# Two attention layers of a decoder on one core: key transfers moved from SyncE to GpSimd, and a causal mask moved from TensorE to VectorE

## The reference

```python
x = x + _L0_attn_ref(_layernorm(x), ...)           # causal, rotary factor on q and k
x = x + _L0_xattn_ref(_layernorm(x), ctx, ctx, ctx)  # a gated feed-forward on the context
x = x + _L0_ffn_ref(_layernorm(x), ...)            # experts
x = x + _L1_attn_ref(_layernorm(x), ...)           # full attention
x = x + _L1_xattn_ref(_layernorm(x), ctx, ...)     # cross attention, softmax over the queries
x = x + _L1_ffn_ref(_layernorm(x), ...)            # experts

def _L0_attn_ref(x, W_attn, b_attn, W_proj, b_proj):
    q, k, v = split(x @ W_attn.T + b_attn)         # 16 heads of 16
    att = (q * f) @ (k * f).T / sqrt(16)
    att = where(tril, att, finfo.min)
    return softmax(att) @ v @ W_proj.T + b_proj
```

## Time and profile before

| | us |
|---|---|
| median of 3 runs (lowest, highest) | 1650.03 (1648.86, 1650.86) |
| the profiled execution's own time | 1650.47 |
| its span | 1648.7 |
| layer 0's attention | about 5 to 280 |
| its context block and experts | 280 to 670 |
| layer 1's self-attention (b = 0 to 3) | 680 to 966 |
| its cross batches (b = 4 to 7) | 966 to 1204 |
| its experts | from 1209 |

### The profile page before, as it was taken

How to read it: one execution, slowest core, us unless ns; L and a number is a source line. 1 busy time by engine, 2 the same in 40 slices (tenths; PEclk the granted TensorE clock), 3 DMA queues, 4 the chain that set the end, 5 groups by cost and what they waited for, 6 DMA issues and landing times. The chain is left out here.

```text
span 1648.7 us, 30586 instructions
## 1 busy us (share of the span) xinstructions
PE 1464.2 (89%) x10430; PEld 1013.4 (61%) x10430; DVE 1165.7 (71%) x2116; ACT 900.5 (55%) x1704; POOL 561.3 (34%) x773
## 2 busy tenths in 40 slices
PE   7899998989899999688999998796965899999996
PEld 3455554559899998333434433232344899999996
DVE  4566553554778887477878759696858688888884
ACT  1354454123256665045666688686922566767662
POOL 6444530010235655545445442021013132333221
PEclk8799999999899999779999999898897999999998
DMA  6222220220258886532223222222133677787772
GB/s 165 50 50 57 47 56 2 73 93 33 103 156 256 255 238 161 133 74 56 57 41 72 55 56 47 61 52 61 40 103 112 221 224 240 240 238 227 252 220 42
DMA packets 104408, 194.48 MB, mean 118 GB/s; under 512 B 30432, under 2 KB 55904, under 8 KB 101312
## 3 DMA queue, kind: packets, MB, share of 16 engines
q1 hardware_dynamic: 75328, 157.91, 30.8%
q0 software_dynamic: 28416, 34.25, 11.9%
q10 hardware_dynamic: 512, 0.40, 0.1%
HBM read 135.76 MB, written 18.61 MB: 94 GB/s over the span
## 5 line engine op out<-in xcount | busy, mean ns | idle before, releaser
L807 ACT ACTIVATE l1a_sb_probs<-l1a_s_ps,l1a_sb_kmax 128x512 f32<-128x512 f32 x256 | 172.4, 700 | 41.4 <-DVE l1a_sb_kmax L740 40.2
L740 DVE TENSOR_REDUCE l1a_sb_kmax<-l1a_s_ps 128x1 f32<-128x512 f32 x256 | 160.5, 676 | 47.8 <-PE l1a_s_ps L932 47.2
L705 DVE TENSOR_REDUCE l1a_sb_mx<-l1a_s_ps 128x2 f32<-128x1024 f32 x128 | 153.4, 1218 | 42.1 <-PE l1a_s_ps L891 42.1
L813 ACT ACTIVATE l1a_sb_probs<-l1a_s_ps 128x1024 f32<-128x1024 f32 x128 | 130.1, 1024 | 85.1 <-PE l1a_s_ps L932 84.8
L932 PEld LDWEIGHTS l1a_s_ps<-l1a_sb_qst,l1a_sb_kst 49*128 49x128 f32 (+1 forms) x512 | 49.8, 193 | 171.5 <-issue 92.7
L705 DVE TENSOR_REDUCE l0a_sb_mx<-l0a_s_ps 128x2 f32<-128x256 f32 (+3 forms) x128 | 103.6, 821 | 72.5 <-PE l0a_s_ps L904 70.9
L2021 PE MATMUL l1m_g_ps<-l1m_sb_rows_hi,l1m_sb_hi 128*128 128x256 f32 x512 | 146.3, 286 | 2.1 <-DVE l1m_sb_late L1919 1.4
L2021 PE MATMUL l1m_g_ps<-l1m_sb_rows_lo,l1m_sb_hi 128*128 128x256 f32 x512 | 144.9, 283 | 0.0
L2021 PE MATMUL l1m_g_ps<-l1m_sb_rows_hi,l1m_sb_lo 128*128 128x256 f32 x512 | 144.9, 283 | 0.0
L932 PE MATMUL l1a_s_ps<-l1a_sb_qst,l1a_sb_kst 49*128 49x512 f32 (+1 forms) x512 | 129.3, 512 | 17.5 <-ACT l1a_sb_probs L807 15.6
L1893 DVE TENSOR_TENSOR l1m_sb_lo<-l1m_sb_raw,l1m_sb_hi 128x512 fp32r<-128x512 f32 x184 | 119.8, 693 | 18.5 <-ACT l1m_sb_hi L1804 17.4
(11 more groups left out here) (409 smaller groups left out, 3967.7 us busy)
## 6 DMA issues: line engine op xcount, KB each, us to landing
l1m_sb_raw<-in_l1m_w SPq DMA_DIRECT2D x92, 512.0 KB, 4.4
l0m_sb_raw<-in_l0m_w SPq DMA_DIRECT2D x72, 512.0 KB, 4.9
l1m_sb_raw<-in_l1m_w SPq DMA_DIRECT2D x23, 1024.0 KB, 6.4
l1a_sb_qst<-l1a_sb_hi SPq DMA_DIRECT2D x256, 32.0 KB, 2.0
l1a_sb_kst<-l1a_sb_hi POOLq DMA_DIRECT2D x156, 32.0 KB, 2.0
l0a_sb_qst<-l0a_sb_hi SPq DMA_DIRECT2D x128, 32.0 KB, 2.2
l1a_sb_qst<-l1a_sb_lo SPq DMA_DIRECT2D x128, 32.0 KB, 2.1
l0a_sb_kst<-l0a_sb_hi POOLq DMA_DIRECT2D x124, 32.0 KB, 2.0
```

What stands on the lines that cost most here:

```text
L705: dve.tensor_reduce(mx[:, g, qt, 2 * p:2 * p + 2], buffer("A", b, g, j)[:, :, 0:last], AX.X, ALU.max).then_inc(a_max.sem, 1)
L740: dve.tensor_reduce(kmax[:, n % 4, e:e + 1], buffer("S", b, g, j)[:, e, :], AX.X, ALU.max, negate=True).then_inc(kmax_done.sem, 1)
L807: ins = act.activation(probs[:, n % 8, e, :], at[:, e, :], ACT.Exp, bias=kmax[:, n % 4, e:e + 1], accum_out=zsum[:, n % 4, e:e + 1])
L813: act.activation(probs[:, n % 8, :, c0:T], at[:, :, c0:T], ACT.Exp, scale=SCALE).then_inc(exp_done.sem, 1)
```

## The change

There are two parts.

The transfers: the step STACK now stands for the queries alone, on SyncE; a new step KEYS, one for each head, issues that head's three key transfers from GpSimd, for all batches (by_sp and its semaphores are gone). In self-attention KEYS stands where STACK stood. The queries' STACK for group 0 of the next batch stands two score steps earlier, at j = 1 of group 1, ahead of M at j = 3. In the cross batches one head's KEYS stands in each of the steps 19 to 30 (groups 0 to 2 of the next batch), and in steps 0 to 3 (group 3 of the running one). CTX stands ahead of the queries' STACK in step 0.

The mask of layer 0: scores_by_query computes scores only. row_max becomes two instructions tensor_tensor_reduce, one for each head: they add a piece of a mask above (128 by 512, f32) to the scores, write the sum to seen (SBUF) and its maximum to mx. The constant mask_q is no longer loaded and cast; above is loaded in its place.

```diff
@@ self_slot
             if g >= 2 and nxt is not None:
                 yield "STACK", nxt, g - 1, 0
+                yield from keys(nxt, g - 1)
...
+        if j == 1 and g == 1 and nxt is not None:
+            yield "STACK", nxt, 0, 0
         if j == 3 and g == 1 and nxt is not None:
-            yield "STACK", nxt, 0, 0
+            yield from keys(nxt, 0)
@@ cross_slot
         if at == 0:
-            yield "STACK", b, NG - 1, 0
             if nxt is not None:
                 if not turned:
                     yield "LN2", nxt, 0, 0
                 yield "CTX", nxt, 0, 0
+            yield "STACK", b, NG - 1, 0
...
+        if at < GH:
+            yield "KEYS", b, NG - 1, at
+        if at >= 19 and nxt is not None and at < 19 + 3 * GH:
+            yield "KEYS", nxt, *divmod(at - 19, GH)
@@ SyncE, stack
-                if by_sp(b):
-                    hi_done.wait(sp, b, i + 1)
-                    lo_done.wait(sp, b, i + 1)
-                    for p in (2 * g, 2 * g + 1):
-                        for e in range(2):
-                            for n, source in enumerate((hi, hi, lo)):
-                                sp.dma_start(in_stack(kst, p, e, n), in_part(source, i + 1, p, e)
-                                             ).then_inc(kstacked_sp[p], 16)
@@ GpSimd
-            def stack(b, g, _):
-                if by_sp(b):
+            def stack(b, g, head):
+                p, e, i = 2 * g + head // 2, head % 2, 2 * (g // 2) + 1
+                if b == 0 and g == 0 and e:
                     return
-                i = 2 * (g // 2) + 1
                 hi_done.wait(pool, b, i)
                 lo_done.wait(pool, b, i)
                 s_ready.wait(pool, b - 1, 8 * g + 7)
-                for p in (2 * g, 2 * g + 1):
-                    for e in range(1 if b == 0 and g == 0 else 2):
-                        for n, source in enumerate((hi, hi, lo)):
-                            pool.dma_start(in_stack(kst, p, e, n), in_part(source, i, p, e)).then_inc(kstacked[p], 16)
+                for n, source in enumerate((hi, hi, lo)):
+                    pool.dma_start(in_stack(kst, p, e, n), in_part(source, i, p, e)).then_inc(kstacked[p], 16)
@@ VectorE, row_max
-                last = (qt + 1) * P if causal else T
-                dve.tensor_reduce(mx[:, g, qt, 2 * p:2 * p + 2], buffer("A", b, g, j)[:, :, 0:last], AX.X, ALU.max
+                if causal:
+                    last = (qt + 1) * P
+                    a_max.wait(dve, b, 8 * g + j - 2)
+                    for e in range(2):
+                        ins = dve.tensor_tensor_reduce(seen[:, j % 2, e, 0:last], buffer("A", b, g, j)[:, e, 0:last],
+                                                       above[:, T - last:T], 1.0, -3e38, ALU.add, ALU.max,
+                                                       mx[:, g, qt, 2 * p + e:2 * p + e + 1])
+                    ins.then_inc(a_max.sem, 1)
+                    return
+                dve.tensor_reduce(mx[:, g, qt, 2 * p:2 * p + 2], buffer("A", b, g, j)[:, :, :], AX.X, ALU.max
                                   ).then_inc(a_max.sem, 1)
@@ TensorE, scores_by_query
-                                    start=True, stop=not causal)
-                if causal:
-                    if b == 0 and g == 0 and j == 0:
-                        pe.wait_ge(const["halved"], 5)
-                    ins = masked(at[:, :, qt * P:last], "mask_q")
+                                    start=True, stop=True)
                 ins.then_inc(a_ready.sem, 1)
```

More of the change, by code:

```diff
@@ L99, in keep_warm, with keys @@
                   start=True, stop=True)
+def keys(b, g):
+    for head in range(GH):
+        yield "KEYS", b, g, head
 def self_slot(kinds, b, g):
@@ L244, in attention_schedule @@
         if use == 3:
-            yield "STACK", 0, 0, 0
-            yield "STACK", 0, 1, 0
+            for g in range(2):
+                yield "STACK", 0, g, 0
+                yield from keys(0, g)
     yield "V", 0, 0, 0
@@ L251, in attention_schedule @@
     yield "STACK", 0, 2, 0
+    yield from keys(0, 2)
     yield "V", 0, 1, 0
     yield "STACK", 0, 3, 0
+    yield from keys(0, 3)
     yield "V", 0, 2, 0
@@ L346, in attention @@
         if causal:
-            halves, before, span = sb("halves", [P, 3, 2, P]), sb("before", [P, P]), sb("span", [P, BLK])
+            halves, before, span = sb("halves", [P, 2, 2, P]), sb("before", [P, P]), sb("span", [P, BLK])
+            above, seen = sb("above", [P, T]), sb("seen", [P, 2, 2, T])
         scores = [ps(f"s_ps{k}", [P, 2, T]) for k in range(3)]
@@ L358, in attention @@
         kstacked = [sem(f"kstacked{p}") for p in range(NPAIR)]
-        kstacked_sp = [sem(f"kstacked_sp{p}") for p in range(NPAIR)] if has_cross else None
         q_scaled = sem("q_scaled")
@@ L446, in attention @@
         STACKED = 6 * 16
-        def by_sp(b):
-            return b > 0 and kinds[b - 1] == "cross"
         def kstack_in(eng, b, p):
-            if by_sp(b):
[L453 to L458, removed]
+            eng.wait_ge(kstacked[p], (b + 1) * STACKED - (STACKED // 2 if p < 2 else 0))
+            if p < 2:
+                eng.wait_ge(kfirst[p], STACKED // 2)
         def stacks_wait(eng, b, i):
@@ L624, in add_bias @@
                                    ).then_inc(v_added.sem, 1)
-            run({"LN1": ln, "LN2": bias, "STACK": stack, "V": v_group, "W": scale_v, "EVAC": add_bias})
+            run({"LN1": ln, "LN2": bias, "KEYS": stack, "V": v_group, "W": scale_v, "EVAC": add_bias})
         @block.vector
@@ L656, in normal @@
                 if causal and b == 0:
-                    dve.wait_ge(const["const_in"], 6 * 16)
-                    for n, half in enumerate(("ident_b", "mask_q", "mask_k")):
+                    dve.wait_ge(const["const_in"], 7 * 16)
+                    for n, half in enumerate(("ident_b", "mask_k")):
                         dve.tensor_copy(const[half][:, :, :], halves[:, n, :, :]).then_inc(const["halved"], 1)
@@ L1006, in load_constants @@
     const["sum0"] = nc.dram_tensor("sum0_dram", (B * T + BLK, D), F32, kind="Internal").ap()
-    for name in ("ident_b", "mask_q", "mask_k"):
+    for name in ("ident_b", "mask_k"):
         sb(name, [P, 2, P], BF16)
@@ L2287, in layout @@
     a["rope"] = np.tile(rope_factor().T, (P // HD, 1))
-    whole = np.stack([a["ident"], np.where(at[None] > at[:, None], NEG, 0),
-                      np.where(at[None] < at[:, None], NEG, 0)]).astype(np.float32)
-    a["halves"] = np.tile(whole.reshape(3, 2, P // 2, P).transpose(2, 0, 1, 3), (2, 1, 1, 1))
+    whole = np.stack([a["ident"], np.where(at[None] < at[:, None], NEG, 0)]).astype(np.float32)
+    a["halves"] = np.tile(whole.reshape(2, 2, P // 2, P).transpose(2, 0, 1, 3), (2, 1, 1, 1))
+    a["above"] = np.where(np.arange(T)[None] - (T - P) > at[:, None], NEG, 0).astype(np.float32)
     large, small = np.arange(NLARGE), np.arange(NSMALL)
```

12 lines of the change are left out of this document (7 added, 5 removed).

## The result

| | median of runs | range, runs | ratio to before, 95% |
|---|---|---|---|
| before | 1649.44 us | 1644.8 to 1650.86, 4 | |
| changed | 1624.93 us | 1616.38 to 1628.05, 4 | 0.9848 [0.9805, 0.9891] |

The change saves 24.5 us (18 to 32 by the interval), where 34 were forecast. The time lies in the stated range, nearer to its middle than to the forecast. The profiled execution took 1623.7 us, its span is 1621.9 against 1648.7, so 26.8 us are to be found in the two traces.

A forecast was written before the change was run, and what follows sets the result against it. It took TensorE to bound layer 0's attention and SyncE's queue layer 1's cross batches. Cross batches -14.8, query transfers -4.2 and layer 0 -15.2 sum to -34.2 us, from 1650.5 to 1616 us; range 1602 to 1640.

The forecast's parts named there:

- 4 to 6. layer 0's masks and maxima: Layer 0: masks off TensorE -20.5 us, new waits +4, prologue maxima +1.3, start's loads 0; together -15.2 us.
- Part 1: Cross batches: with key transfers off SyncE, both stalls for ctxT and the slow products behind them go, gaining 22.8 us.
- Part 2: Cross batches: key issues on GpSimd delay the scalings of V, so TensorE loses 2.7 us in each of three, +8 us.
- 16 heads in 17 steps: Cross batches: sixteen heads' issues plus GpSimd's own work make 31.8 us in 28.4 us, so scalings come late.
- Part 3: First batch of each layer: query transfers two steps earlier remove TensorE's waits of 3.17 and 2.75 us; -4.2 us together.
- Part 4: Layer 0: 512 mask matmuls leave TensorE, 0.22 us for each of 93 tiles with another matmul behind, -20.5 us.
- Part 5: Layer 0: VectorE's maxima become additions with running maximum and accumulator reads, +0.23 us a tile, 4 us of new waits.
- rival 5: Layer 0: VectorE's addition with maximum runs at half rate, +0.88 us a tile, 1659 us in all; chance 0.09.

The follow-up runs named there:

- e6: The kernel before with ctxT's load ahead of the last group's transfers in SyncE's queue, all keys still on SyncE; 1644.3 us.
- e7: The changed kernel with ctxT's load behind the last group's query transfers again, keys still on GpSimd; 1621.3 us.
- e10: The changed kernel with the next batch's first query group back at step 3 of the second group, in both self-attentions; 1627.1 us.
- e1: The kernel before with the transfers' part of the change alone, masks by query staying on TensorE; 1631.5 us.
- e9: The changed kernel with the third group's four key heads, behind a cross batch, in steps 5, 7, 9, 11 instead of 27 to 30; 1613.3 us.
- e2: The kernel before with the masks' part of the change alone, transfers as before; 1640.7 us.
- e11: The changed kernel without the four masks by key behind each score tile by key in layer 0; timed once, 1617.6 us.
- e8: The kernel before with each tile's four masks by query issued twice in layer 0; 1661.5 us.
- e4: The changed kernel with the last group's key heads in steps 13, 15, 17, 18 and the third group's, behind a cross batch, in 5, 7, 9, 11; 1609.0 us.

## Why the prediction was right, and where its terms were off

| term | forecast | in the two traces |
|---|---|---|
| 1. stalls for ctxT | -22.8 | -22.2 |
| 2. GpSimd delays the scalings | +8 | +8.5 |
| 3. first query transfers | -4.2 | -9.7 |
| 4 to 6. layer 0's masks and maxima | -15.2 | -7.9 |
| the rest | 0 | +4.5 |
| sum | -34.2 | -26.8 |

**Part 1** was right in mechanism and size: -11.05 and -11.14 us at the two places, the slow product behind each wait included. e6 and e7 show that it is the queue's length.

**Part 2** was right in mechanism and, by these landmarks, in size: 2.9, 4.3 and 1.3 us at the three boundaries, 8.5 in all, against 2.7 each. In e10's trace it is 8.6, in e1's 10.3. The scaling at 1012.25 stood at 1021.48 before; the products around it had moved by 13.8 us, so it is 4.6 us late, where I had laid it 4.2 late (its step 32, 31 in the code). That the sum agrees is in part luck. The three boundaries differ by a factor of three, and TensorE's waits for vscaled are 12.2 us, which took the place of waits for ScalarE and of slow products that I hadn't counted. The forecast's cause, "16 heads in 17 steps", was half wrong: only four of them do it, and by e9 they can go elsewhere. 31.8 us of work in 28.4 is an average; what counts is which issues stand ahead of which scaling.

**Part 3** was mis-sized by more than half: 4.2 for 9.7. I took about 1 us off the waits for row transfers behind them, and counted the waits alone. The clock falls behind these waits as it does behind those for ctxT, so 5.1 and 4.6 us went (e10 loses 5.8 and 4.7 with waits somewhat longer). The trace before had the row for it, the key product of 3.29 us that starts 3.2 us behind the end of the wait, in place of 1.98. A row transfer does come late in that batch, by 0.69 us at 75.00; another, by 0.73 at 232.29, isn't due to the order (e2, with the transfers as before, waits 0.85 there).

**Part 4** is the term that was missed: 0.22 us a mask where 0.13 was to be had. I divided the 0.22 us from masks to product by looking for a tail behind unmasked scores, and took it from layer 1 (0.32 us), where a score by query stands behind another score. In layer 0 masks by key stand ahead of it, and there the tail is 0.40. (Without these e11 shows 0.33 ahead of a transpose but 0.38 ahead of a projection, so what stands ahead is only a part of the difference.) e8 says the same from the other side: 0.11 a set. Over the 80 tiles from 88.91 to 237.04 TensorE's time without its waits fell by 8.7 us: 148.1 less 3.4 of waits, against 142.1 less 6.1. That is 0.11 a tile, or 0.13 where a product follows and little elsewhere. The waits rose by 2.7 us in these tiles (ScalarE's by 1.7, VectorE's by 1.0), near the 4 that I put down for the whole stretch.

**Part 5.** Full rate, so rival 5 is out: 0.687 us at 512 columns. The Trainium skill's Vector Engine (DVE) Microarchitecture Reference, section "7. Points that are easy to get wrong", states the halving for two SBUF sources that aren't bf16. Here one is in PSUM, and the trace agrees; what two SBUF sources would cost no run here shows. The pair costs 0.09 us a tile at 512 columns, not 0.23, because the read of the accumulator hides: the low end of my bounds (+0.04) was nearly right, and the value that I took wasn't.

**The rest.** At the end of layer 0's attention the clock fell at another point than before, and two output projections ran at half clock:

```profile
272.40 2.04 PE L989 MATMUL l0a_m_ps<-l0a_sb_wout,l0a_sb_oT 128*128 128x256 f32 x4 [0.88 <-DVE x_sb L736]
```

They took 1.10 us each before, so 1.9 us. Another 2.9 us are the half-clock stretch at 989 in the first cross batch; the other places give back 0.3. At the end of layer 1's attention TensorE stands longer before its next stage:

```profile
PE l1m_g_ps L98 <- PEq L304: 5.0, 1, 5.0
```

It was 1.9 us before. All kernels with the keys on GpSimd show 3.9 to 5.0, all with them on SyncE (before, e2, e6, e8) 1.9. It costs nothing in the sum: a third of it is given back within 20 us, and the end of the span is as far ahead (26.8 us) as the last output projection (26.7). What TensorE's sequencer waits for isn't shown by any run; that remains open.

The forecast thus came out 7.4 us too fast in the traces: 7.3 from layer 0's masks, 0.5 from GpSimd, 0.6 from the stalls and 4.5 from the rest, and 5.5 the other way from part 3. Part of its agreement is errors that cancel: layer 0's term was about twice too large, the term of the first query transfers less than half of what it measured.

## What to carry to other kernels

When the issues of a batch take their queue longer than the batch lasts, reordering them moves the stall (e6: 19.7 us became 20.1 elsewhere) and taking issues away removes it. Work that is put on a helper engine costs by what it stands in front of: see which instruction of that engine each consumer waits for, and put the new ones just behind it; four heads' issues a batch at the wrong steps cost some 10 us here (e4 against the changed kernel), and some steps later next to nothing that the landmarks show. Price an instruction that is to be removed by doubling it in the same place, since a row from a place with other neighbours had 0.08 us less of tail. Look behind each wait for products at half clock, and look whether the same products ran at half clock without it.
